# Staging one weight piece later and cutting the last batch's norm and routing work into smaller portions on VectorE, in an attention and mixture-of-experts kernel

## The reference

```python
x = x + layernorm(attention(layernorm(x), wq, bq, wk, bk, wv, bv, wo, bo))   # 16 heads of 16, causal mask
x = x + layernorm(ffn(layernorm(x), Ws, bs, Wg, Wu, Wd))
# ffn: logits = x @ Ws + bs; the two best of 8 experts by token, softmax over the two
#      y = (silu(x @ Wg[e]) * (x @ Wu[e])) @ Wd[e]   with 256 -> 688 -> 256, summed with the two weights
```

## Time and profile before

| | us |
|---|---|
| three runs | 891.24, 889.12, 882.86 |
| profiled execution | 878.99 (span 877.2) |
| PE busy | 713.8 (81%) |
| DVE busy | 615.1 (70%) |
| ACT busy | 550.6 (63%) |
| POOL busy | 444.1 (51%) |
| mean granted PE clock | 0.917 |

### The profile page before, as it was taken

How to read it: one execution, slowest core, us unless ns; L and a number is a source line. 1 busy time by engine, 2 the same in 40 slices (tenths; PEclk the granted TensorE clock), 3 DMA queues, 4 the chain that set the end, 5 groups by cost and what they waited for, 6 DMA issues and landing times.

```text
span 877.2 us, 21718 instructions
## 1 busy us (share of the span) xinstructions
PE 713.8 (81%) x6822; PEld 470.2 (54%) x6822; DVE 615.1 (70%) x1960; ACT 550.6 (63%) x1122; POOL 444.1 (51%) x552
## 2 busy tenths in 40 slices
PE   3677677768777989988997899898979999999920
PEld 1244444444443355544554455466857888888810
DVE  5777898888877878897889778755744445444445
ACT  4588885857765667756676576565545555555536
POOL 3554433553624435664577457747564343343427
PEclk9689998998986599999999899999999999999965
DMA  6434231463251111221122021213345233232257
GB/s 194 139 118 147 91 115 44 147 191 108 94 174 49 35 31 21 44 55 20 20 43 52 11 32 38 53 23 56 50 99 145 44 43 45 44 46 42 38 138 268
DMA packets 74008, 69.09 MB, mean 79 GB/s; under 512 B 6832, under 2 KB 67888, under 8 KB 73904
## 3 DMA queue, kind: packets, MB, share of 16 engines
q1 hardware_dynamic: 60624, 53.23, 19.7%
q0 software_dynamic: 13280, 14.49, 11.6%
HBM read 34.04 MB, written 31.29 MB: 74 GB/s over the span
## 4 chain that ended last, share of the span: by engine, by line
PE 46%; DVE 31%; issue 8%; ACT 7%; POOL 5%; DMA 2%; SPq 0%; DVEq 0%; POOLq 0%; ACTq 0%
PE bank L1880 13%; PE bank L1902 10%; PE bank L1724 6%; DVE nmax L1149 5%; DVE unused L1162 5%; PE bank L1631 4%; PE bank L1742 3%; DVE stats L1115 3%; DVE stage L1338 2%; POOL gu_part L862 2%; DVE rows L1130 2%; PE bank L1662 2%; DVE gu_part L1364 2%; PE bank L1591 2%; PE bank L1618 1%
## 5 line engine op out<-in xcount | busy, mean ns | idle before, releaser
L983 ACT ACTIVATE pT<-bank 128x512 f16<-128x512 f32 (+1 forms) x384 | 200.0, 534 | 97.3 <-PE bank L1631 95.0
L759 POOL TENSOR_SCALAR_AFFINE_SELECT pT<-pT 128x512 f16<-128x512 f16 x128 | 87.9, 731 | 146.2 <-ACT pT L983 145.9
L1149 DVE TENSOR_REDUCE nmax<-bank 128x1 f16<-128x384 f32 (+2 forms) x216 | 126.2, 597 | 35.6 <-PE bank L1620 33.6
L1880 PE MATMUL bank<-tile_xT,gu_part 128*128 128x256 f16 (+1 forms) x1100 | 132.4, 275 | 6.9 <-DVE stage L1450 3.6
L1880 PEld LDWEIGHTS bank<-tile_xT,gu_part 128*128 (+1 forms) x1100 | 106.5, 100 | 29.9 <-issue 8.4
L1162 DVE CUSTOM_DVE_ANT_0 unused<-bank,mask 128x384 f16<-128x384 f32 (+2 forms) x224 | 103.5, 483 | 16.5 <-PE bank L1609 15.1
L1450 DVE SCALAR_TENSOR_TENSOR stage<-bank,stage 128x512 f32<-128x512 f32 (+1 forms) x100 | 55.5, 555 | 80.4 <-ACT stage L1036 70.4
L785 POOL DMA_INDIRECT expert_rows<-tile_y,tile_dest x52 | 83.4, 1603 | 55.0 <-ACT tile_y L968 46.4
L1902 PE MATMUL bank<-wd_part,stage 128*128 (+2 forms) x850 | 105.3, 277 | 2.5 <-ACT stage L1045 1.7
L1724 PE MATMUL bank<-tile_xT,gu_part 128*128 128x256 f16 (+1 forms) x616 | 90.2, 286 | 12.8 <-DVE stage L1346 12.3
L1902 PEld LDWEIGHTS bank<-wd_part,stage 128*128 128x128 f16 (+2 forms) x850 | 78.2, 99 | 23.4 <-issue 13.8
(11 more groups left out here) (201 smaller groups left out, 1433.2 us busy)
## 6 DMA issues: line engine op xcount, KB each, us to landing
expert_rows<-tile_in SPq DMA_DIRECT2D x8, 1024.0 KB
stage<-wg SPq DMA_DIRECT2D x8, 688.0 KB, 4.0
stage<-wu SPq DMA_DIRECT2D x8, 688.0 KB, 4.2
stage<-wd SPq DMA_DIRECT2D x8, 640.0 KB, 4.2
tile_in<-dispatch_rows SPq DMA_DIRECT2D x39, 130.0 KB
gu_part<-expert_rows SPq DMA_DIRECT2D x16, 256.0 KB, 6.1
out<-gu_part SPq DMA_DIRECT2D x16, 256.0 KB, 2.4
x_sb<-x SPq DMA_DIRECT2D x8, 256.0 KB
```

What stands on the lines that cost most here:

```text
L759: last = gp.affine_select(out=diagonal, in_=diagonal, compare_op=ALU.is_ge, fill=0.0, base=0, pattern=[[0, J], [1, P]], channel_multiplier=-1)
L983: sc.activation(pT[:, lo:hi], ST_BANK[i % 2][:, 0:hi - lo], ACT.Exp, scale=1.0 / INV_SCALE).then_inc(p_ready, 1)
L1149: v.tensor_reduce(columns, S_BANK[i % 2][:, 0:n * len(heads)].rearrange("p (j n) -> p j n", n=n), AX.X, ALU.max, negate=True).then_inc(s_m ...
L1880: last = mm(target, keep["gu"][part][:, bass.ds(col + (kd * GU + at), width_)], tile_xT[(WOVEN + m) % 2][:, kd, :], start=(s == 0), stop=( ...
```

## The change

`EARLY` goes from 5 to 4. Piece 4 (a wd piece) moves into head group 0 and each later piece moves one place on; group 12 now has a piece of its own. `POOLED` has 8 pieces rather than 9. On DVE, `beside` places the same portions behind other blocks. On PE, the wait for `const_ready` moves from ahead of the first projection to ahead of the first scores. The lists of PE's gap, of POOL, of SP and of ACT's gap are as they were.

```diff
-        EARLY = 5
+        EARLY = 4
         HELD = 3 * (E - 1)
-        PIECES_OF = [2] * G + [1] * (2 * G) + [0] * G + [2, 1]
+        PIECES_OF = [2] * G + [1] * (2 * G + 1) + [0] * (G - 1) + [2, 1]
...
                     if m == 0 and n == NB - 1:
-                        for at in range(0, 4):
+                        for at in range(0, 2):
+                            finish(B - 1, 3 * B - 2, at)
+                    if m == 1 and n == 0:
+                        for at in range(2, 4):
                             finish(B - 1, 3 * B - 2, at)
                     if m == 1 and n == NB - 1:
-                        for at in range(4, 10):
+                        for at in range(4, 7):
+                            finish(B - 1, 3 * B - 2, at)
+                    if m == 2 and n < 2:
+                        for at in ((7, 8), (9,))[n]:
                             finish(B - 1, 3 * B - 2, at)
                     if m == 2 and n == NB - 1:
                         for at in range(10, 12):
                             finish(B - 1, 3 * B - 2, at)
                     if m == 3 and n == NB - 1:
-                        for at in range(len(AT_ROUTE)):
+                        for at in range(0, 3):
+                            route(B - 1, at)
+                    if m == 4 and n == 0:
+                        for at in range(3, 6):
                             route(B - 1, at)
                         dve.wait_ge(later_consts, 6)
                         v.tensor_copy(pads.bitcast(U32)[:, :, :, D // 2], pad_ids)
                     if m == 4 and n == 1:
-                        for at in range(len(AT_SLOTS)):
+                        for at in range(0, 2):
+                            slots(B - 1, at)
+                    if m == 4 and n == 2:
+                        for at in range(2, 4):
                             slots(B - 1, at)
                         wait_taken(dve, ("ranks", B - 1))
                         v.tensor_copy(fill_u, keep["fill"][:, :]).then_inc(pad_ready, 1)
-                    if m == 4 and n >= 2:
-                        later(n - 2)
-                    if m == 5 and n < 2:
-                        later(n + 2)
+                    if m == 4 and n == NB - 1:
+                        later(0)
+                    if m == 5 and n < NB - 1:
+                        later(n + 1)
...
                 pe.wait_ge(w_in, 16 * 10)
-                pe.wait_ge(const_ready, 1)
                 wait_taken(pe, ("xnT", 0))
...
                 wait_taken(pe, ("q", G - 2))
+                pe.wait_ge(const_ready, 1)
                 first_scores(0)
```

## The result

The changed kernel takes **892.06 us** (median of 12 runs, 888.35 to 895.54). The kernel before, run beside it, takes 882.57 us (median of 12, 879.98 to 891.24). The ratio is 1.0086, 95% interval 1.0060 to 1.0113: slower by 0.9%, just inside the 1% that the forecast called no change. The step is 9.5 us by the medians and 7.9 us by the means (892.05 against 884.14), which lie nearer the ratio. The forecast of 892.0 us met the number, but not the step. It added 3 us to 889.1, a median of three runs that lies 6.5 us above the later one of twelve: that the two errors cancel is luck. The profiled execution after took 889.22 us (span 887.5) against 878.99 (span 877.2): +10.2.

The account below looks back on a forecast made before the run. No engine full over the span: lead-in bound by waits for POOL, piece 4 and DVE, gap by PE and POOL's tile chain. Terms -4.4 + 0.7 + 6.0 + 0.8 + 0 + 0.6 = +3.7 us; 889.1 + 3 = 892 us, range 884 to 898.

Parts of the forecast that it names:

- +6.0 us at tile 18: Gap: POOL's later second root delays SP's load, so PE transposes tile 18 6.0 us later, bounds +4.4 and +6.8.
- my margin of 2.4 us: Gap: time between tile 17's landing at 618.0 us and its transposes on PE at 620.45 us in the old profile.
- The second costs 1.2 us: Gap: slower clock after the wait for tile 18 costs 1.2 us, two chances in three, counted as +0.8 us.
- The first fall costs nothing: Gap: a clock fall after the wait for tile 17 adds 0, since tile 18 is later anyhow.
- Net 0: Gap, m = 4: column 2 starts 2.5 us later, split slots remove stalls of 1.51 and 0.8 us; bounds -1 and +2.5.
- m = 5: +0.6: Gap, m = 5: the last later portion ahead of the last low block delays down products 0.6 us, bounds 0 and +1.
- outer bound of -5.5: Lead-in: largest gain expected from both edits together, if PE, less idle, reaches its higher clock earlier.
- -4.4 forecast: Lead-in: earlier constants and piece 4 moved out together save 4.4 us, bounds -3.4 and -5.5.
- +0.7: Group 12: the sixteenth DVE piece placed there costs 0.7 us, bounds 0 and 2.7 us.
- rival C: Lead-in gain does not survive batch 0, DVE limits; front worth -0.7, total +9.6 us, 899 us; chance 0.12.
- Forecast A: Likeliest case: POOL's list, held by two later var_ready, loses more than the lead-in gains; +0 to +7 us; chance 0.58.
- Rival B: Gap nearly neutral: first delay shrinks to 2.5 us, second to the margin; -4 to -1 us overall; chance 0.23.

Follow-up runs that it names:

- e4: Changed kernel with the ten norm portions back at their old places, routing, slots and later staying new: 877.58 us, ratio 1.0026 to the kernel before.
- e7: Changed kernel with routing, slots and later back at their old places, norm portions staying new: 881.58 us, ratio 1.0092 to the kernel before.
- e6: Changed kernel with POOL's list reordered, stores and takes ahead of the roots, DVE's list unchanged: 878.94 us, ratio 1.0046 to the kernel before.
- e11: Changed kernel with routing, slots and later at old places and POOL's stores and takes ahead of its roots: 879.35 us, ratio 0.9982 to the kernel before.
- e2: Kernel before with only PE's wait for the constants moved to the first scores: 876.41 us, ratio 1.0006.
- e1: Kernel before with only four early pieces and the new share of pieces by group: 877.41 us, ratio 1.0014.
- e5: Kernel before with both lead-in edits, four early pieces and the later wait for constants, gap as before: 875.22 us, ratio 1.0003.
- e8: Kernel before with the changed lead-in and, of the gap's changes, only the split of slots and later: 876.08 us, ratio 1.0009.
- e3: Kernel before with only the new places of DVE's norm, routing, slot and later portions, lead-in as before: 885.50 us, ratio 1.0123.
- e9: Kernel before with the changed lead-in, but DVE's sixteenth piece in group 14 instead of 12, gap as before: 880.60 us, ratio 0.9970.
- e12: e9 plus the slots of e8 and POOL's second root moved behind the issue of store 15: 878.42 us, ratio 0.9971 to the kernel before.

## Why the prediction was right in its number and short in its step

**The chain in the gap was right.** DVE's portions hold `var_ready`, that holds POOL's root, its stores and takes, then SP's load, then PE. e4 and e7 separate it, and e6 and e11 cut it at POOL: the waits for both tiles vanish. The forecast had +6.0 us at tile 18 (bounds 4.4 to 6.8); e7 against e2 shows 47.3 - 42.0 = 5.3. As forecast, the second root rules: it comes 34.4 us after the last exponential in e7, 28.6 in e2 (+5.8), the first only 21.7 against 19.1 (+2.6). I had taken the first from a trace in which PE stood still in m = 1; in e1, e2, e4, e5 and e8 tile 17 is awaited already in the old order (1.04 us in e4), so my margin of 2.4 us was that stall, not slack.

**The step that failed in the gap is the clock, "The second costs 1.2 us", counted at +0.8.** From tile 18 to tile 19, e7 needs 14.3 us and e2 11.6: +2.7, with no wait that e2 lacks. The row behind the wait for tile 18 shows why: the down products take 6.56 us in e7 and 6.54 in e3 instead of 4.08, at a granted clock of 0.50, the lower level, 1.2 GHz. In the changed kernel they take 5.66 us at 0.58. So this wait costs itself and then 1.6 to 2.5 us more, not 0.8.

"The first fall costs nothing" did hold. In the changed kernel the clock falls behind the wait for tile 17 as well (5.75 us at 0.57), and the wait for tile 18 is shorter by it (2.02 us, 3.66 in e3): from tile 17 to 18 it takes 13.3 us, and 13.2 in e3, where no such fall came. Nor does every wait bring a fall: behind 2.84 us in e3 and 2.91 in e7 the down products ran in 4.08 us.

In the 100 us behind the last exponential the lower level was granted for 0 us in e2, 6.8 in e7, 10.2 in e3, and 6.8 before against 20.5 after. Of 6.56 us at the lower level the down products of e7 lose 2.48 (6.56 - 4.08). At that rate the 13.7 us more on the profiled pair are worth some 5 us, an estimate. Only 10.2 of the 20.5 lie behind the three waits. The other 10.3, like the 6.8 before, lie at the stalls of the last section, which are no part of the change. The Trainium skill, TensorE: Matmul & The Clock Gate, Part 1: The HAM clock gate (the "warmup" mystery), says that idle lets the array fall back to the throttled state. The rows agree at each of the three waits of the changed kernel, and show no fall at the first wait of e3 and e7.

**m = 4: "Net 0" was too kind.** The forecast had column 2 late by 2.5 us: the wait went from 1.34 to 3.84, exactly that. It had 2.3 us back from the slots, and the down products indeed run through, 4.44 us with no stall. But the clock is low behind the wait of 3.84 us: column 2 takes 2.61 us, not 1.63, and part of the down products runs slow (in e3 column 2 runs in 1.73 us and the down products take 5.32). e4 against e2: +3.7 at tile 19, +1.8 at the end of the gap. **m = 5: +0.6** isn't seen: from tile 19 to 21 e3 takes 23.0 us, e2 23.8.

**The lead-in: right where it was forecast, gone at the end.** Behind head group 11 the changed kernel is 5.5 us ahead in its trace (group 12 starts at 203.4 us, 208.9 before), at the forecast's outer bound of -5.5. Over all traces the mean start of group 12 is 204.9 us with this lead-in and 209.1 with the old one, 4.2 us, near the -4.4 forecast. "+0.7" for the piece in group 12 was low: the group lasts 14.5, 14.0 and 13.9 us without it (before, e2, e3), and 14.9 to 16.2, mean 15.8, with it (after, e1, e4 to e8, e11), +1.6. The trace of before had part of the price: group 8, at the same place with a piece, lasts 15.5 us. At the last exponential the eight kernels with this lead-in stand at 581.4 to 590.5 us, mean 585.9; the three with the old one at 585.5 to 586.8, mean 586.1. So almost nothing of the 4.2 us is left in the mean, and e5 times it at 1.0003 [0.9969, 1.0037], 2.7 us faster to 3.2 slower. The piece in group 12 takes 1.6, and at group 16 the mean lead is 2.9 us. The rest goes between groups 16 and 31, where the traces differ by up to 9 us and the lower clock comes and goes. Which cause makes that is open; no run here fixed the clock. This is the largest miss of the forecast: it counted -3.7 us for the lead-in to the end of the kernel and gave no reason why the later groups would keep it. That the gain does not survive was rival C, but not as I put it: not in batch 0, and not by DVE there.

**The balance.**

| term | forecast, us | measured, us | by |
|---|---|---|---|
| lead-in with its piece | -3.7 | +0.3 (-2.7 to +3.2) | e5 |
| tile 18 | +6.0 | +5.3 | e7 against e2 |
| clock behind it | +0.8 | +2.7 | the same |
| m = 4 and 5 | +0.6 | +1.8 | e4 against e2 |
| sum | +3.7 | about +10 | |

The measured step is 9.5 us by the medians and 7.9 by the means (interval of the ratio: 5.3 to 10.0 us). The profiled pair reaches the last exponential 3.2 us apart, so the lead-in may be worth up to that in single executions. Forecast A reached to +7: the step lies at or beyond its bound, and the likeliest case was right in the mechanism of the gap and low in size. Rival C's +9.6 is the nearest step, with another cause for the lost lead-in. Rival B was right that the first delay could shrink to 2.5 us (2.6 in e7), but not in the second: both roots are late in each trace that has the new norm order and POOL's old list. Rival D fell with e3.

## What to carry to other kernels

Price a new wait of PE at its length plus a possible slow stretch of the matmuls behind it. Here that was 0 to 2.5 us for waits of 2.0 to 3.8 us, and it differed between kernels with the same wait. A slow stretch that a later wait for a DMA contains costs nothing, as in the forecast. A margin read from one profile is worth only as much as the absence of other stalls in that stretch: compare like steps (tile with tile, group with group of the same place) before calling time idle or slack. A gain early in a long pipeline should be followed to the end of the stage by a run of that part alone, since here some 4 us were ahead after a third of the batches and nearly none at their end.

## What the runs showed of the hardware

**PE starved without a releaser.** In before, after and e9 to e12 PE loses 3 to 5 us at m = 0 or 1 and 2 to 5 us more at m = 5 or 6, mostly with "issue" as the reason; e1 to e8 hold none of this (tile 16 is transposed 20.4 to 20.7 us after the last exponential in them, and 23.2 to 25.9 us in the six). At m = 5 of the changed kernel ACT stands for 3.64 us with no releaser that the profile can name, and PE waits 4.40 us behind it. e9 to e12 all ran on one chip and e1 to e8 on the other two, so chip or session may decide it, and not the kernel. Timelines of PE, e9 with the stall (the view ends at 611 us), then e8 without it, at the same work:

```profile
606.33 0.27 PE L1880 MATMUL bank<-tile_xT,gu_part 128*128 128x256 f16 x1 [0.16 <-issue]
607.03 1.12 PE L1880 MATMUL bank<-tile_xT,gu_part 128*128 128x256 f16 x6 [0.43 <-issue]
609.18 2.08 PE L1880 MATMUL bank<-tile_xT,gu_part 128*128 128x256 f16 x9 [1.03 <-issue]
```
```profile
597.11 5.04 PE L1883 MATMUL bank<-tile_xT,gu_part 128*128 128x256 f16 x44
```

POOL issues the indirect DMAs of the scatter meanwhile in both, and no instruction DMA shows in e9 between 603 and 612 us. The cause is open. The gap is 3.5 us longer in the trace of before than in e2's, and 8 us longer in that of after than in e3's, more than most terms of the forecast. In the changed kernel the stall falls ahead of the second half of the norm's statistics, and POOL's first root comes 27.0 us after the last exponential (21.7 in e7); before, it falls behind them, and the root comes at 19.0 (19.1 in e2). That this makes the difference between 3.5 and 8 us is argued, not tested.

**A tiny operation held by POOL.** DVE's ws_r step of 128 x 16 takes 2.62 us in the changed kernel, from 34.78 to 37.40 us, and 0.17 us at 37.87. POOL's low part of 128 x 1280 runs from 34.76 to 37.37 us. The Trainium skill, SBUF — State Buffer, SBUF: two separate sides, calls the port pair of the two engines an exclusive lock, held for a whole instruction. These times fit that; no run here takes the two apart. It is also what the earlier exponentials ran into, since the maximum that PE awaits for 3.58 us stands behind this step in DVE's list.
